# Two DRAM tables in turn for the block additions of a macaron layer, merged afterwards, and a new order of stages

## The chip, the core and the metric

The program runs on one core of a Trainium2 chip. The metric is device time in microseconds (us) of one execution, the median of the runs shown. The engines are named as in the profile: PE (TensorE, matrix products), DVE (VectorE), ACT (ScalarE), POOL (GpSimd, which here also issues the DMAs that add into memory or take row numbers) and SP (SyncE, which issues the plain DMAs).

## The reference

A layer in three parts on x of shape (4, 512, 512): half of a mixture of experts, an attention-like part with running sums over the sequence, and half of the same mixture again. Cut to what matters:

```python
x = x + 0.5 * ffn(layernorm(x))       # 8 experts, best 2 of each row, and a shared one
x = x + attn(layernorm(x))
x = x + 0.5 * ffn(layernorm(x))

# ffn: gates of the best two experts of a row
routed = sum_e gates[n, e] * (gelu(xf @ w1[e] + b1[e]) @ w2[e] + b2[e])
shared = gelu(xf @ sw1 + sb1) @ sw2 + sb2
# attn (batch of 512 rows, 32 heads, 8 angles of each): z = conv4(x @ W_mem), q = x @ W_q
# p = exp(score + decay); cs = cumsum([p, p*cos(k*theta), p*sin(k*theta)]); out = cs . q / den
# y = out_re @ W_re + out_im @ W_im; y = y_val * silu(y_gate); return y @ W_out
```

## The kernel before

All of it stands in one function, `macaron`. The four batches of 512 rows are walked as eight **jobs** q (four for the first mixture, four for the second) and four **groups** g of two batches (groups 0 and 1 belong to the first mixture, 2 and 3 to the second).

A job loads its rows (`fetch`), normalises them (`load`, `norm`), turns them for PE (`turn`, L722), makes the gate logits and ranks them, and computes the shared expert: `hidden` (L757) and then `acc` (L767, L769). `add_shared` (L1589) adds each tile of the shared result into the sum in DRAM, with an adding DMA from POOL.

A group then sends its 2048 (row, expert) pairs to 23 **blocks** of 128 pairs, each of one expert. `scatter` (L1557, 16 DMAs) writes the lists. Block j is brought by its row numbers into one of the NX = 2 tiles `xs` (`bring_rows`, L1569), turned (L801), multiplied by w1 (L810), turned again (L818), put through gelu on ACT (L991), multiplied by w2 (L826), scaled into one of two tiles `ys` (`keep_sums`, L1004) and added to its rows in DRAM by number (`add_rows`, L1582). Two blocks can hold the same row (a row has two experts), and so the additions of a group form a **chain**: `add_rows` of block j waits until that of block j-1 has landed, by the semaphore `y_added`, and the first of a group waits for the shared results. For the first mixture the table added to is `x1_rows` (which begins as a copy of x, L1803), for the second it is `out` (which begins as a copy of `x1_rows`, L1767, `begin_output`).

Between the mixtures stands attention, batch by batch. The head (`a_load` L1719, `a_stats`, `a_turn` L834, `a_mem` L845, `a_q` L854, `a_spread`) is followed by 16 steps on DVE (`c_turn`, `c_scan` L1374, `c_times` L1381 and L1386, `c_sum`), whose queries are loaded two steps ahead by SP into `qx` and whose sines come from ACT (L1072 to L1075); then `c_out` (L867), `o_gate` (L879) and `o_rows` (L888), whose tiles POOL adds into `x1_rows` (L1594). `kval` keeps the keys of 2 * HALVES = 4 halves.

Nothing is scheduled on the chip. `orders()` lays all stages of all engines in one order when the program is built: it runs a plan in which each `piece` has a length, the pieces that it comes after (with a time to landing for DMAs) and the banks that it needs, and takes for each engine the stage with the longest way to the end; the DVE steps come last among DVE's stages. Each engine's program is that order, with waits on semaphores. An engine that waits holds all that stands behind it.

## Time and profile before

| what | us |
|---|---|
| median of 3 runs (lowest, highest) | 1291.89 (1288.80, 1291.98) |
| the profiled execution, device time | 1298.13 |
| its span in the trace | 1296.8 |
| busy PE, DVE, ACT, POOL | 1005.9, 719.3, 594.9, 447.9 |

The profiled execution took 1.3 us beside its span, and was 6.2 us longer than the median. The profile page gives the busy time of each engine, the span in 40 slices, the chain of work that ended last (followed back from the last instruction through what released each step) and the costliest groups of instructions. The trace behind it gives each instruction with its start, and what ended the idle time before it. A share of busy time is an average over stages with different limits, and so the stages are read one by one: the blocks of group 0 (105 to 234 us), a long middle in which attention and groups 1 and 2 share the engines (to about 1045 us), the last attention product (to 1091 us), the last job (to 1152 us) and the blocks of group 3, alone, to the end.

### The profile page before, as it was taken

What the parts mean: (1) busy time and instruction counts of PE and PEld (TensorE: products, weight loads), DVE (VectorE), ACT (ScalarE), POOL (GpSimd) and SP (SyncE); (2) the same over time, 40 slices, a digit from 0 to 9 for tenths busy, and PEclk for the clock granted to TensorE, in tenths of its full rate; (3) what the DMA queues carried; (4) which work ended last, traced back from release to release, by engine and by line L of the source; (5) the groups of instructions that cost most, each with busy time, mean ns of one, the idle gap of its engine ahead of it and who ended that gap; (6) DMA issues with size and microseconds to landing.
All of it is one profiled execution on the core that took longest, in us unless ns stands there. A gap on an engine that the chain in (4) does not pass through costs nothing.

```text
span 1296.8 us, 10501 instructions
## 1 busy us (share of the span) xinstructions
PE 1005.9 (78%) x3168; PEld 538.4 (42%) x3168; DVE 719.3 (55%) x1162; ACT 594.9 (46%) x1015; POOL 447.9 (35%) x432
## 2 busy tenths in 40 slices
PE   6999889964986768887983569976986796969774
PEld 3446555422443434453431234454453442436542
DVE  3401000087888695987898989997996830200000
ACT  4334333333535575567532345376758720413332
POOL 4263443203634343232110134344452312244442
PEclk9999989986988897888896869988998998889997
DMA  8974554424156465486143742665676435035454
GB/s 283 377 188 87 101 86 69 78 84 124 30 108 177 95 124 107 105 234 157 49 111 85 175 139 47 153 151 129 124 189 146 78 49 106 33 74 96 92 90 55
DMA packets 60587, 155.13 MB, mean 120 GB/s; under 512 B 10962, under 2 KB 10962, under 8 KB 58358
## 3 DMA queue, kind: packets, MB, share of 16 engines
q0 software_dynamic: 29568, 60.90, 27.7%
q1 hardware_dynamic: 30966, 93.58, 23.8%
q8 instruction: 27, 0.44, 0.1%
q14 instruction: 26, 0.21, 0.1%
HBM read 99.74 MB, written 58.88 MB: 122 GB/s over the span
## 4 chain that ended last, share of the span: by engine, by line
DMA 32%; PE 32%; DVE 12%; ACT 8%; issue 7%; POOL 7%; SPq 1%; POOLq 0%; ACTq 0%; DVEq 0%
DMA x_rows<-ys,into_i 12%; DMA out_rows<-ys,into_i 11%; PE hps L757 6%; PE yps L769 6%; PE misc L888 4%; DMA xs<-x_normal,rows_i 4%; PE yps L826 3%; PE hps L810 3%; POOL slots L1557 3%; DVE run L1374 2%; PE misc L854 2%; DMA xin<-in_x 2%; ACT ys L1004 2%; PE misc L845 1%; ACT xin L1025 1%
## 5 line engine op out<-in xcount | busy, mean ns | idle before, releaser
L826 PE MATMUL yps<-w_all,hidden_sb 128*128 x368 | 202.5, 679 | 57.2 <-ACT hidden_sb L991 56.8
L810 PE MATMUL hps<-w_all,hidden_sb 128*128 x736 | 186.6, 400 | 1.2 <-ACT hidden_sb L974 1.1
L1374 DVE TENSOR_TENSOR_SCAN run<-pwx,trig 128x512 f32<-128x512 f32 x128 | 149.4, 1208 | 61.8 <-ACT trig L1075 61.3
L810 PEld LDWEIGHTS hps<-w_all,hidden_sb 128*128 128x128 f32 x736 | 145.4, 204 | 44.9 <-issue 27.4
L1569 POOL DMA_INDIRECT xs<-x_normal,rows_i x92 | 111.3, 1210 | 91.9 <-PE xps L801 65.2
L1004 ACT ACTIVATE ys<-yps,slots 128x512 f32<-128x512 f32 x92 | 62.9, 685 | 169.3 <-PE yps L826 72.3
L1582 POOL DMA_INDIRECT x_rows<-ys,into_i x46 | 79.4, 1727 | 169.6 <-ACT ys L1004 81.7
L1582 POOL DMA_INDIRECT out_rows<-ys,into_i x46 | 82.7, 1798 | 155.4 <-DMA out_rows<-ys,into_i 79.6
L826 PEld LDWEIGHTS yps<-w_all,hidden_sb 128*128 128x128 f32 x368 | 73.9, 213 | 128.7 <-issue 126.5
L757 PE MATMUL hps<-xnT,sw_sb 128*128 128x512 f32 x256 | 121.3, 623 | 3.2 <-ACT hidden_sb L964 1.7
L801 PE MATMUL xps<-ident,xs 128*128 128x128 f32 x368 | 60.7, 297 | 77.4 <-DMA xs<-x_normal,rows_i 75.9
L769 PE MATMUL yps<-sw_sb,hidden_sb 128*128 128x512 f32 x256 | 118.4, 605 | 0.0
L1557 POOL DMA_INDIRECT slots<-told,dest_i x64 | 70.1, 1096 | 63.0 <-DVE cmp_a L1244 28.2
L888 PE MATMUL misc<-turns_sb,tail_sb 128*128 128x512 f32 x192 | 86.8, 608 | 5.3 <-DVE tail_sb L1435 5.3
L722 PE MATMUL xps<-ident,xin 128*128 128x128 f32 x128 | 26.1, 359 | 80.5 <-ACT xin L1025 74.2
L801 PEld LDWEIGHTS xps<-ident,xs 128*128 128x128 f32 x368 | 45.9, 151 | 97.9 <-DMA xs<-x_normal,rows_i 59.2
L1381 DVE TENSOR_TENSOR trig<-run,qx 128x1024 f32<-128x1024 f32 x64 | 78.0, 1219 | 5.7 <-DMA qx<-q_cols 5.4
L1290 DVE BATCH_NORM_STATS2 stats_attn<-xin 128x6 f32<-128x512 f32 x16 | 10.6, 688 | 121.7 <-DMA xin<-x_rows 121.5
L1386 DVE TENSOR_TENSOR qx<-run,qx 128x1024 f32<-128x1024 f32 x64 | 77.9, 1217 | 0.0
L757 PEld LDWEIGHTS hps<-xnT,sw_sb 128*128 128x128 f32 x256 | 49.5, 200 | 67.4 <-issue 63.7
L1072 ACT ACTIVATE trig<-trig 128x512 f32<-128x512 f32 x64 | 40.4, 631 | 72.4 <-DVE trig L1363 72.2
L974 ACT COPY hidden_sb<-xps 128x512 f32<-128x512 f32 x92 | 53.1, 594 | 35.5 <-PE xps L801 33.9
(199 smaller groups left out, 1531.3 us busy)
## 6 DMA issues: line engine op xcount, KB each, us to landing
qx<-q_cols SPq DMA_DIRECT2D x128, 256.0 KB
x_normal<-xin SPq DMA_DIRECT2D x32, 256.0 KB, 3.8
w_all<-in_w_experts SPq DMA_DIRECT2D x8, 1024.0 KB, 9.8
xin<-x_rows SPq DMA_DIRECT2D x32, 256.0 KB, 6.5
turns_sb<-in_w_out SPq DMA_DIRECT2D x3, 1536.0 KB, 7.5
xin<-in_x SPq DMA_DIRECT2D x16, 256.0 KB, 4.2
x_rows<-ys POOLq DMA_DIRECT2D x16, 256.0 KB, 4.5
q_cols<-xin SPq DMA_DIRECT2D x16, 256.0 KB
```

Source lines behind the costliest of these rows:

```text
L757: t = PE.matmul(hps[:, bank, :], sw1_sb[:, c, n * P:(n + 1) * P], xnT[:, c, :], start=c == 0, stop=c == KC - 1)
L769: t = PE.matmul(yps[:, bank, :], hT[:, n, tb * P:(tb + 1) * P], sw2_sb[:, n, :], start=False, stop=n == SC - 1)
L801: t = PE.transpose(xps[:, bank, c * P:(c + 1) * P], xs[:, j % NX, c * P:(c + 1) * P], ident[:, :])
L810: t = PE.matmul(hps[:, bank, 0:H], xT[:, j % 2, c, :], w_all[:, bass.ds(expert[j] + c * H, H)], start=c == 0, stop=c == KC - 1)
L826: t = PE.matmul(yps[:, bank, :], hb[:, j % 2, ec, :], w_all[:, bass.ds(expert[j] + (KC * H + ec * D), D)], start=ec == 0, stop=ec == EC - 1)
L888: t = PE.matmul(misc[:, bank, :], yT[:, v, tb * P:(tb + 1) * P], wout_sb[:, v, :], start=v == 0, stop=v == VT - 1)
L1004: SE.activation(ys[:, j % 2, :], yps[:, bank, :], ACT.Copy, scale=slots[:, g % 2, j, 1:2]).then_inc(*ys_kept.of((g, j)))
L1374: t = VE.tensor_tensor_scan(run[:, c, :], pwx[:, n // M, :], trig[:, n % 2, c, :], 0.0, ALU.mult, ALU.add)
L1381: VE.tensor_tensor(trig[:, n % 2, :, :], run[:, :, :], qx[:, n % NQX, :, :], ALU.mult).then_inc(*real_made.of((b, n)))
L1557: GE.indirect_dma_start(slots_dram[g], bass.IndirectOffsetOnAxis(dest_i[:, g % 2, t, r:r + 1], 0), told[:, g % 2, t, r, :], None).then_inc ...
L1569: GE.indirect_dma_start(xs[:, j % NX, :], None, xn_rows[g % 2], bass.IndirectOffsetOnAxis(rows_i[:, g % 2, j:j + 1], 0)).then_inc(*xs_load ...
L1582: GE.indirect_dma_start(INTO[g], bass.IndirectOffsetOnAxis(into_i[:, g % 2, j:j + 1], 0), ys[:, j % 2, :], None, compute_op=ALU.add).then_ ...
```

## The change

**Two tables.** The even blocks of a group add into `x1_rows`, by `rows_i`, and the odd blocks into a second table, by `into_i`: the new `sum_rows` for the first mixture, `out` for the second. Each side has its own semaphore, and `add_rows` of block j waits for block j-2 instead of j-1. The shared results are no longer added: `store_shared` writes them, as plain stores from SP, as the first content of the second table. The copy of `x1_rows` to `out` is gone.

**Merging.** For attention each row tile is loaded from `x1_rows` as before, and then POOL adds the tile of `sum_rows` onto it in SBUF (`add_sums`, four DMAs a batch). `merge_rows` adds a batch of `sum_rows` into `x1_rows` for those who read it later (1 MB, from DRAM to DRAM). At the end of groups 2 and 3 `merge_output` adds the batches of `x1_rows` into `out`, one adding DMA of 1 MB a batch; the end of the program waits for them, and in group 3 the first odd block waits for the two of group 2.

**Room.** There are three `xs` tiles instead of two, so a block can be brought three ahead, and in exchange `kval` keeps three halves instead of four.

**The order.** The lengths in the plan are set anew. PE: `turn` and `a_turn` 0.8 to 0.7, `chunks` 1.6 to 1.3, `logits` 1.3 to 0.9, `acc` 4.4 to 4.2, `x` 0.8 and 2.0 to 0.7 and 1.9, `one` and `two` 2.0 to 1.9, `a_mem` 4.1 to 3.7, `a_q` 4.1 to 3.8, `a_spread` 1.2 to 0.8, `o_gate` 2.5 to 1.9, `o_rows` 5.5 to 5.3. POOL: `bring` 1.0 to 1.2, `add` 1.6 to 1.8 with a landing of 3.8 instead of 3.4. With the changed waits this moves instructions on every engine.

```diff
-        NX, NR = 2, 2
+        NX, NR = 3, 2
...
-        NK = 2 * HALVES
+        NK = 3
...
+        sum_rows = [nc.dram_tensor(f"sum_rows{i}", (GR + P, D), F32).ap() for i in range(2)]
...
-        SUM = [x1_rows if f == 1 else out for f, _ in JOBS]
-        INTO = [x1_rows[g] if g < 2 else out_rows for g in range(NG)]
+        SUM = [sum_rows if f == 1 else out for f, _ in JOBS]
+        INTO = [(x1_rows[g % 2], sum_rows[g % 2] if g < 2 else out_rows) for g in range(NG)]
...
-                piece("PE", s, 4.4, ("DVE", ("gT", q)), ("ACT", ("hidden", q, SC - 1)), *start[1:2],
+                piece("PE", s, 4.2, ("DVE", ("gT", q)), ("ACT", ("hidden", q, SC - 1)), *start[1:2],
...
-                piece("POOL", s, 1.0, ("ACT", s), ("SP", ("w_rows" if f == 1 else "w_out", b), 8.0))
+                piece("SP", s, 0.5, ("ACT", s), *([("POOL", ("add", g - 1, NB - 1), 3.8)] if g == NG - 1 else []))
...
-                piece("POOL", ("bring", g, j), 1.0, ("DVE", ("rows", g)), ("SP", ("norm", a), 2.5), ("SP", ("norm", z), 2.5),
+                piece("POOL", ("bring", g, j), 1.2, ("DVE", ("rows", g)), ("SP", ("norm", a), 2.5), ("SP", ("norm", z), 2.5),
...
-                last = [("POOL", ("add", g, j - 1), 3.4)] if j else []
-                if j == 0:
-                    last = [("POOL", ("acc", z, tb), 3.6) for tb in range(TB)]
-                    last += [("POOL", ("add", g - 1, NB - 1), 3.4)] if g else []
-                piece("POOL", ("add", g, j), 1.6, ("ACT", s), *last)
+                      ("POOL", ("add", g, j - 2), 3.8) if j >= 2 else ("SP", ("acc", z, TB - NR + j), 3.6))
+                if j >= 2:
+                    last = [("POOL", ("add", g, j - 2), 3.8)]
+                elif j == 1:
+                    last = [("SP", ("acc", q, tb), 3.6) for q in (a, z) for tb in range(TB)]
+                    last += [("POOL", ("m_out", b), 10.0) for b in range(GB)] if g == NG - 1 else []
+                else:
+                    last = [("SP", ("w_rows", JOBS[q][1]), 12.0) for q in (a, z)] if g < 2 else []
+                piece("POOL", ("add", g, j), 1.8, ("ACT", s), *last)
+            if g >= 2:
+                for q in (a, z):
+                    piece("POOL", ("m_out", JOBS[q][1]), 1.0, ("POOL", ("add", g, NB - 1), 3.8),
+                          ("POOL", ("add", g, NB - 2), 3.8))
...
+            for tb in range(TB):
+                piece("POOL", ("a_add", b, tb), 1.0, ("SP", ("a_load", b), 3.6 - 0.6 * (TB - 1 - tb)))
+            piece("POOL", ("m_rows", b), 1.0, ("POOL", ("a_add", b, TB - 1)))
+            piece("DVE", ("a_stats", b), 3.4, *[("POOL", ("a_add", b, tb), 3.8 - 0.8 * (TB - 1 - tb)) for tb in range(TB)])
...
+        def blocks_added(g):
+
+            return [y_added[side].at((g, NB - 1 - (NB - 1 - side) % 2)) for side in range(2)]
...
             def add_rows(g, j):
 
+                side = j % 2
                 pool.wait_ge(*ys_kept.at((g, j)))
-                if j > 0:
-                    pool.wait_ge(*y_added.at((g, j - 1)))
+                if j >= 2:
+                    pool.wait_ge(*y_added[side].at((g, j - 2)))
                 elif g > 0:
-                    pool.wait_ge(*y_added.at((g - 1, NB - 1)))
-                for i in range(NR):
-                    pool.wait_ge(*acc_added[i].at((GB * g + 1, TB - NR + i)))
-                GE.indirect_dma_start(INTO[g], bass.IndirectOffsetOnAxis(into_i[:, g % 2, j:j + 1], 0),
-                                      ys[:, j % 2, :], None, compute_op=ALU.add).then_inc(*y_added.of((g, j)))
-            def add_shared(q, tb):
-                f, b = JOBS[q]
-                pool.wait_ge(*acc_kept.at((q, tb)))
-                pool.wait_ge(*rows_begun[q].at(q))
-                GE.dma_start(row_tile(SUM[q], b, tb), ys[:, tb % NR, :],
-                             accum_op=ALU.add).then_inc(*acc_added[tb % NR].of((q, tb)))
+                    for end in blocks_added(g - 1):
+                        pool.wait_ge(*end)
+                if j == 0 and g < 2:
+                    for q in (GB * g, GB * g + 1):
+                        pool.wait_ge(*rows_begun[JOBS[q][1]].at(JOBS[q][1]))
+                elif j == 1:
+                    for i in range(NR):
+                        pool.wait_ge(*acc_stored[i].at((GB * g + 1, TB - NR + i)))
+                    if g == NG - 1:
+                        for b in range(GB):
+                            pool.wait_ge(*out_merged[b].at(b))
+                at = into_i if side else rows_i
+                GE.indirect_dma_start(INTO[g][side], bass.IndirectOffsetOnAxis(at[:, g % 2, j:j + 1], 0),
+                                      ys[:, j % 2, :], None, compute_op=ALU.add).then_inc(*y_added[side].of((g, j)))
+            def add_sums(b, tb):
+                pool.wait_ge(*a_loaded[tb].at(b))
+                pool.wait_ge(*blocks_added(b // GB)[1])
+                GE.dma_start(xin[:, tb, :], row_tile(sum_rows, b, tb), accum_op=ALU.add).then_inc(*a_summed[tb].of(b))
+            def merge_rows(b):
+                for tb in range(TB):
+                    pool.wait_ge(*a_loaded[tb].at(b))
+                GE.dma_start(batch_rows(x1_rows, b), batch_rows(sum_rows, b),
+                             accum_op=ALU.add, max_dma_last_dim=4096).then_inc(*rows_merged[b].of(b))
+            def merge_output(b):
+                for end in blocks_added(2 + b // GB):
+                    pool.wait_ge(*end)
+                GE.dma_start(batch_rows(out, b), batch_rows(x1_rows, b), accum_op=ALU.add,
+                             max_dma_last_dim=4096).then_inc(*out_merged[b].of(b))
...
-                sp.wait_ge(*y_added.at((b // GB, NB - 1)))
+                sp.wait_ge(*blocks_added(b // GB)[0])
...
-            def begin_output(b):
-                for i in range(2):
-                    sp.wait_ge(*row_added[i].at((b, TB - 2 + i)))
-                if b == B - 1:
-                    sp.wait_ge(*y_added.at((NG - 2, NB - 1)))
-                SP.dma_start(batch_rows(out, b), batch_rows(x1_rows, b)).then_inc(*rows_begun[B + b].of(B + b))
+            def store_shared(q, tb):
+                b = JOBS[q][1]
+                sp.wait_ge(*acc_kept.at((q, tb)))
+                if q == NJ - 1:
+                    for end in blocks_added(NG - 2):
+                        sp.wait_ge(*end)
+                SP.dma_start(row_tile(SUM[q], b, tb), ys[:, tb % NR, :]).then_inc(*acc_stored[tb % NR].of((q, tb)))
...
-                sp.wait_ge(*acc_added[i].at(acc_added[i].order[-1]))
-            sp.wait_ge(*y_added.at((NG - 1, NB - 1)))
+                sp.wait_ge(*acc_stored[i].at(acc_stored[i].order[-1]))
+            for end in blocks_added(NG - 1):
+                sp.wait_ge(*end)
+            for b in range(B):
+                sp.wait_ge(*out_merged[b].at(b))
```

POOL at the end of the program, before: the additions (L1582) stand all in `out_rows`.

```order
262 L1582 DMA out_rows<-ys,into_i 2048x512
263 L1569 DMA xs<-x_normal,rows_i 128x512
264 L1582 DMA out_rows<-ys,into_i 2048x512
265 L1569 DMA xs<-x_normal,rows_i 128x512
266 L1582 DMA out_rows<-ys,into_i 2048x512
267 L1569 DMA xs<-x_normal,rows_i 128x512
268 L1582 DMA out_rows<-ys,into_i 2048x512
269 L1569 DMA xs<-x_normal,rows_i 128x512 x2
270 L1582 DMA out_rows<-ys,into_i 2048x512 x6
```

The same place after (L1614 is `add_rows`, L1590 `bring_rows`, L1632 `merge_output`).

```order
293 L1614 DMA out_rows<-ys,into_i 2048x512
294 L1614 DMA x_rows<-ys,rows_i 1152x512
295 L1590 DMA xs<-x_normal,rows_i 128x512
296 L1614 DMA out_rows<-ys,into_i 2048x512
297 L1614 DMA x_rows<-ys,rows_i 1152x512
298 L1614 DMA out_rows<-ys,into_i 2048x512
299 L1614 DMA x_rows<-ys,rows_i 1152x512
300 L1614 DMA out_rows<-ys,into_i 2048x512
301 L1614 DMA x_rows<-ys,rows_i 1152x512
302 L1632 DMA out_rows<-x_rows 256x1024 x2
```

The two tables take turns, and two merges of 1 MB stand behind the last addition.

PE at the end of group 2, before: the w2 product of the last block (L826), then `hidden` of job 6 (L757) with `c_out` of the last attention half (L867) in its midst, then `acc` of job 6 (L767, L769) and `o_gate` (L879) in turn.

```order
1187 L826 MATMUL yps<-w_all,hidden_sb 128x512
1188 L757 MATMUL hps<-xnT,sw1_sb 128x512 x4
1189 L740 MATMUL xps<-chunk_sum,chunks_sb 128x8 x4
1190 L757 MATMUL hps<-xnT,sw1_sb 128x512 x4
1191 L867 MATMUL misc<-low_rows,rep_sb 128x512
1192 L757 MATMUL hps<-xnT,sw1_sb 128x512 x4
1193 L749 MATMUL xps<-ident,gcols 27x128 x4
1194 L757 MATMUL hps<-xnT,sw1_sb 128x512 x4
1195 L767 MATMUL yps<-bias_parts 128x512
1196 L769 MATMUL yps<-sw2_sb,hidden_sb 128x512 x4
1197 L879 MATMUL misc<-outT,wbd_sb 128x512
1198 L879 MATMUL xps<-outT,wbd_sb 128x512
```

The same place after, from the last block's product (L845) on: `hidden` is L776, `c_out` L886, `acc` L786 and L788.

```order
1195 L845 MATMUL yps<-w_all,hidden_sb 128x512
1196 L752 MATMUL xps<-xnT,gate_sb 32x512 x4
1197 L776 MATMUL hps<-xnT,sw1_sb 128x512 x8
1198 L759 MATMUL xps<-chunk_sum,chunks_sb 128x8 x4
1199 L776 MATMUL hps<-xnT,sw1_sb 128x512 x8
1200 L768 MATMUL xps<-ident,gcols 27x128 x4
1201 L886 MATMUL misc<-low_rows,rep_sb 128x512
1202 L786 MATMUL yps<-bias_parts 128x512
1203 L788 MATMUL yps<-sw2_sb,hidden_sb 128x512 x4
```

All of `hidden` now stands ahead of `c_out`, and all four tiles of `acc` stand ahead of the `o_gate` products, which come after the rows shown.

## Rows read from the trace of the kernel before

**Rows 1.** The page, part 4: the chain that ended last, by line.
```profile
DMA x_rows<-ys,into_i 12%; DMA out_rows<-ys,into_i 11%; PE hps L757 6%; PE yps L769 6%; PE misc L888 4%; DMA xs<-x_normal,rows_i 4%; PE yps L826 3%; PE hps L810 3%; POOL slots L1557 3%; DVE run L1374 2%; PE misc L854 2%; DMA xin<-in_x 2%; A
```
**Rows 2.** Timeline of POOL, additions of group 3: start us, us, engine, operation [idle <-releaser].
```profile
1167.38 1.65 POOL L1582 DMA_INDIRECT out_rows<-ys,into_i  x1 [2.30 <-ACT ys L1004]
...
1281.70 1.55 POOL L1582 DMA_INDIRECT out_rows<-ys,into_i  x1 [4.04 <-DMA out_rows<-ys,into_i]
...
1292.21 1.55 POOL L1582 DMA_INDIRECT out_rows<-ys,into_i  x1 [3.66 <-DMA out_rows<-ys,into_i]
```
**Rows 3.** Timeline of ACT, the last scaling of a block into ys.
```profile
1286.34 0.69 ACT L1004 ACTIVATE ys<-yps,slots 128x512 f32<-128x512 f32 x1 [4.62 <-DMA out_rows<-ys,into_i]
```
**Rows 4.** Groups by line in 1167 to 1290 us: count, busy us, mean ns, idle before, releasers.
```profile
L826 PE MATMUL yps<-w_all,hidden_sb 128*128 x88 | 42.1, 602 | 9.4 <-ACT hidden_sb L991 9.4
L1569 POOL DMA_INDIRECT xs<-x_normal,rows_i x18 | 17.9, 996 | 7.5 <-issue 4.9 <-PE xps L801 2.6
L801 PE MATMUL xps<-ident,xs 128*128 128x128 f32 x80 | 12.0, 285 | 12.1 <-DMA xs<-x_normal,rows_i 11.4 <-issue 0.6
```
**Rows 5.** Windows: stretch, its us, then busy (count) of PE, PEld, DVE, ACT, POOL, clock.
```profile
105.00:220.00 115.00, 99.84 (x391) 65.30 (x390) 3.57 (x24) 46.87 (x110) 51.36 (x39) 0.94 0.49 87
1156.70:1281.20 124.50, 102.56 (x414) 68.62 (x414) 0.00 (x0) 46.43 (x114) 52.69 (x41) 0.97 0.48 87
270.00:1045.00 775.00, 582.92 (x1735) 301.07 (x1734) 662.41 (x942) 424.87 (x675) 254.03 (x204) 0.87 0.52 122
```
**Rows 6.** Timeline of PE in group 3: one block without waits, and PE's last products.
```profile
1259.34 0.66 PE L801 MATMUL xps<-ident,xs 128*128 128x128 f32 x4 [1.59 <-DMA xs<-x_normal,rows_i]
1259.83 0.38 PE L818 MATMUL hps<-ident,hidden_sb 128*128 128x128 f32 x2
...
1263.49 0.38 PE L818 MATMUL hps<-ident,hidden_sb 128*128 128x128 f32 x2
...
1277.54 3.69 PE L826 MATMUL yps<-w_all,hidden_sb 128*128 x8 [0.31 <-ACT hidden_sb L991]
```
**Rows 7.** Timeline of POOL and ACT: two additions issued together, and who waited for each.
```profile
1144.45 1.94 POOL L1589 DMA_DIRECT2D out_rows<-ys  x2
...
1149.09 0.60 ACT L1018 ACTIVATE ys<-yps 128x512 f32<-128x512 f32 x1 [10.61 <-DMA out_rows<-ys]
1150.46 0.60 ACT L1018 ACTIVATE ys<-yps 128x512 f32<-128x512 f32 x1 [0.77 <-DMA out_rows<-ys]
```
**Rows 8.** DMA issues: operation, count, KB each, median us from issue to landing.
```profile
x_normal<-xin SPq DMA_DIRECT2D x32, 256.0 KB, 3.8
x_rows<-ys POOLq DMA_DIRECT2D x16, 256.0 KB, 4.5
x_rows<-in_x SPq DMA_DIRECT2D x4, 15.0
out_rows<-x_rows SPq DMA_DIRECT2D x4, 8.2
```
**Rows 9.** Timeline of PE after group 0; attention's loads: durations ns, first and last start.
```profile
219.85 13.90 PE L757 MATMUL hps<-xnT,sw_sb 128*128 128x512 f32 x32
...
246.66 0.60 PE L834 MATMUL misc<-ident,xin 128*128 128x128 f32 x4
...
L1719 SPq DMA_DIRECT2D xin<-x_rows x16: 319/379/387, 233.7 to 762.7; - x16
```
**Rows 10.** Waits of DVE in 394 to 620 us: total us, times, longest.
```profile
DVE run L1374 <- ACT trig L1075: 37.2, 9, 11.9
DVE trig L1381 <- DMA qx<-q_cols: 3.7, 1, 3.7
```
**Rows 11.** Timeline after group 2: PE's hidden and last attention product, DVE's last step.
```profile
1031.10 3.60 PE L757 MATMUL hps<-xnT,sw_sb 128*128 128x512 f32 x8
...
1069.71 20.76 PE L888 MATMUL misc<-turns_sb,tail_sb 128*128 128x512 f32 x48
...
1044.79 1.38 DVE L1419 SCALAR_TENSOR_TENSOR tail_sb<-outT,small_sb,misc 128x512 f32<-128x512 f32 x2
```

95 lines of the change are left out of this document (52 added, 43 removed).

## The prediction

> **What bounds the kernel now.** I read the chain that ended last first [rows 1]: 12% of the span is additions into x_rows on their way to landing, 11% additions into out_rows, some 300 us of 1296.8. No engine has such a share. It lies mostly in groups 0 and 3, where little or nothing of attention runs beside the blocks.
>
> The last blocks show the mechanism. The 23 additions of group 3 start 5.67 us apart (22 intervals in 1292.21 - 1167.38 [rows 2]). Of this an addition takes 4.6 us from its start to landing at the very end (the one from 1281.70 lets ACT go at 1286.34 [rows 2, 3]); ACT's copy into ys, 0.69 [rows 3], or as much time on POOL, passes until the next begins, some 0.8 in all, so a landing is 4.9 on average. What PE needs itself is far less. At 1259 to 1263 us [rows 6] it runs a block without a wait: 0.49 us for the turning (1259.34 to 1259.83) and 3.66 from one L818 to the next (which holds L818, L810 and L826), so **4.15 us a block** against 5.67. It was done at 1281.2, while the additions ended at 1296.8 [rows 2, 6]. The time in groups 0 and 3 is that of the chain.
>
> In the middle DVE is busy 662.4 of 775 us and PE 582.9 [rows 5]. There DVE is the tightest engine, and a chain that gets shorter gives back only what DVE idles for.
>
> **Group 3, additions in two tables.** Two additions may be under way at once. A pair then needs one landing and one ACT copy: 4.9 + 0.8 = 5.7 us for two blocks, 2.85 a block. POOL needs 1.6 for an addition, 1.0 for a bring and two gaps of 0.3 (4.9 us for issue ahead of the brings), together 3.2 [rows 2, 4]. Both lie under PE's 4.15, so PE is late next. Its waits in this stretch were 11.4 us for the brought rows and 9.4 us for gelu [rows 4]. The third xs tile and the freed POOL take the first away; the second (9.4 / 22 = 0.43 a block) I keep, since gelu still stands between two products of a block. That is 4.15 + 0.43 = 4.58 us a block. PE's busy time over the same 23 blocks is 102.6 / 23 = 4.46 [rows 5], more than 4.15 because in a run with gaps the end of each piece counts; 4.46 + 0.43 = 4.89. I take the middle, **4.7**. Before, PE took 124.5 us for the 23 blocks [rows 5]; after, 23 x 4.7 = 108.1, a gain of 16.4. Behind PE the additions took 15.6 us (1281.2 to 1296.8); now one copy (0.1 + 0.69) and one landing (4.6), 5.4, a gain of 10.2. **Sum 26.6.** Bounds: at 4.15 a block 39; at 5.1 (if the new order of PE meets ACT more often) 17.
>
> Do two additions really overlap? Two of the shared additions were issued 0.97 us apart (1.94 for two) [rows 7]; those who waited went on at 1149.09 and 1150.46, 1.37 us apart and not a landing of 4.6.
>
> **The last merge.** New, behind everything: two adding DMAs of 1 MB from DRAM to DRAM, after a wait on POOL (0.8). No row has it. The nearest is the plain copy of the same 1 MB between the same tables, 8.2 us [rows 8]. The adding form costs the same as the plain one at 256 KB (4.5 with POOL's longer issue, against 3.8) [rows 8]. From 256 KB to 1 MB, 4.4 us more for 0.75 MB is 5.9 us a MB, so the second merge adds 5.9: 0.8 + 8.2 + 5.9 = **15 us lost.** Bounds: both hidden in one another, 9; each like the slowest kind of 1 MB copy in the trace, 15.0 [rows 8], one after the other, 31. I take 15, because the chip does nothing else then, as at the 8.2.
>
> The Trainium skill, DMA: Bandwidth & Descriptors, section Anatomy of one DMA, has for a DMA issued by GpSimd 2.0 us and then 436 KB a us, an estimate of 6.8 us for these 2 MB. By it the sum would be 8 us better. The trace speaks against it: the 1 MB copy took 8.2 where the rule has 4.4 [rows 8].
>
> **Group 0.** The same chain, but PE had other work among the blocks: it was busy 99.8 of 115 us and idle 15.2 [rows 5], and right behind it stand hidden and acc of job 2, on PE alone, from 219.85 until attention's rows are turned (the first at 246.66) [rows 9]. So only PE's idle counts. I keep a third of it: **gain 10** (5 to 15). The new add_sums (about 4.5 us, like the 256 KB addition [rows 8]) stands between the last addition and attention's first row. It is hidden: PE has 26.8 us of hidden and acc from the end of the blocks to the first turned row, while a copy and landing (5.4), add_sums (5) and the 13 us from attention's first load (233.7) to that row [rows 9] make 23.4. If that cover went, it would cost up to 5.
>
> **Shared results, copies, kval.** The 32 shared additions leave POOL (about 1 us each, mostly in its idle time) and become stores on SP; four copies of 1 MB go and four merge_rows come, off the path. A third kval half makes a_mem of half 1 wait for steps of the batch before, which PE's order already has behind them. I cost these at nothing; the cover of all three is DVE's 85% busy middle.
>
> **The middle.** Between 394 and 620 us DVE waited 37.2 us for ACT's sines [rows 10]; ACT stood in order behind the blocks. A shorter chain takes part of that, but the same ACT work is packed closer. I take 4 us (-12 to 30). At the end of group 2 hidden ran only from 1031.10, the end of the blocks, and the last attention product began at 1069.71, while DVE was done at 1046.2 [rows 11]. PE had 38 us of work, of which hidden (four times 3.6) would fit ahead of DVE's end if the blocks end sooner. Up to 14 us; DVE limits it as well, I take 4. **Gain 8.**
>
> **The sum.** 26.6 - 15 + 10 + 8 = 29.6 us. Against the profiled execution, 1298.1 - 29.6 = 1268.5; that was 6.2 above the median, so 1291.9 - 29.6 = 1262.3, say **1262**.
>
> **Rivals.**
> 1. The middle gives much: DVE's 37.2 us mostly return, 30 instead of 4, and group 3 runs at 4.4 a block (7 us). 1262 - 26 - 7 = **1229**. For it: a third of the chain on the additions lies in the middle. Against: DVE at 85%.
> 2. The gain in the middle is eaten. The new order was laid for other lengths than those under load, and add_sums stands in three more heads: between 0 and -12 for the middle instead of 8, which gives 1270 to 1282, and **1282** at the end. For it: POOL and DMA are slower there than at the ends.
> 3. The merges cost 31 and more and the middle gives nothing: 1291.9 - 26.6 - 10 + 31 = **1286**, and from 33 us on it is no change.
> 4. Slower, by SP's queue. The shared stores now stand among the query loads in SP's order, and each waits for ACT's copy of a product of PE. If PE is late, the load behind is late and with it DVE. Twelve such stores (jobs 3, 4 and 5) stand in the middle, and a load is about one step of DVE ahead. The wait for queries is 3.7 us today [rows 10]. It decides when the twelve hold DVE for more than 34 / 12 = 2.8 us each; at 4 us, 1262 + 48 = **1310**.
> 5. The change doesn't do what it says: additions of one queue land one after another whatever the semaphore. Then groups 0 and 3 keep 5.67 us and the merges come on top: 1291.9 + 15 - 8 = **1299**. The pair in [rows 7] speaks against it.
>
> **Chances.** Forecast (1248 to 1274) 0.56; rival 1 (below) 0.14; rival 2 (above, to 1284) 0.18; rival 3 0.04; rival 4 0.05; rival 5 0.03. A measurement of this kernel can tell about 0.3%, 3.9 us, from no change. Faster by more: 0.56 + 0.14 + 0.18 and half of rival 3, 0.90; within 0.02; slower 0.08. The range goes from the middle of rival 1 and the forecast to the end of rival 2: 1240 to 1284.
>
> **What would show it.** Additions of group 3 starting less than 4.8 us apart, in pairs of tables, with PE's wait for xs gone and its last product some 5 us before the last landing; at the end two merges of together about 15 us; PE's end of group 0 at about 210 instead of 220; the wait of DVE for trig below 37 us. The prediction is wrong if PE's own waits for ACT grow with the new order, if the merges cost 30, or if DVE shows new waits for qx.

## The result, and the profile after

The changed kernel took **1239.45 us** (1235.05 to 1244.39, 4 runs) against 1290.35 for the kernel before beside it: a ratio of 0.961 (95% interval 0.956 to 0.966), 50.9 us less. The forecast was 1262, 29.6 less, with a range from 1240: the direction was right and the gain was forecast much too small. The profiled execution took 1235.89 us, with a span of 1234.6.

The page of the changed kernel, the chain that ended last by engine and by line:

```profile
PE 46%; DVE 15%; DMA 12%; ACT 12%; POOL 7%; issue 7%; SPq 1%; POOLq 0%; DVEq 0%; ACTq 0%
PE yps L845 10%; PE hps L829 9%; PE hps L776 7%; PE yps L788 6%; PE misc L907 6%; POOL slots L1578 4%; DVE run L1395 2%; DMA outT<-tail_sb 2%; DMA x_rows<-tail_sb 2%; PE misc L873 2%; DMA x_rows<-ys,rows_i 2%; ACT xin L1045 2%; DVE trig L1402 1%; DMA q_cols<-xin 1%; PE misc L864 1%
```

The additions on their way to landing, 23% of the span in [rows 1], are down to some 2%. What stands first now is PE's work on the blocks, L845 and L829 (L826 and L810 before).

The timeline of POOL in group 3: start, us, engine and line, operation, and in brackets the idle time before it with its releaser.

```profile
1118.34 1.64 POOL L1614 DMA_INDIRECT x_rows<-ys,rows_i  x1 [3.69 <-ACT ys L1023]
...
1123.24 1.58 POOL L1614 DMA_INDIRECT out_rows<-ys,into_i  x1 [1.97 <-ACT ys L1023]
...
1127.66 1.58 POOL L1614 DMA_INDIRECT x_rows<-ys,rows_i  x1 [0.30 <-issue]
...
1216.47 1.55 POOL L1614 DMA_INDIRECT x_rows<-ys,rows_i  x1 [1.91 <-ACT ys L1023]
1221.67 1.93 POOL L1632 DMA_DIRECT2D out_rows<-x_rows  x2 [3.65 <-DMA x_rows<-ys,rows_i]
```

Against [rows 2]: tables in turn, and 4.46 us from one addition to the next (22 intervals in 1216.47 - 1118.34) instead of 5.67. From the first block to the merges' issue POOL's additions wait 31.6 us for ACT's copy and only 5.3 for a landing; before it was 34.8 and 31.9. The end is new: the two merges are issued at 1221.67 and the span ends at 1234.6, 12.9 us later. POOL had waited for the last addition up to then.

Four stretches of the changed kernel, then three of the kernel before. Columns: stretch, its us, then busy us (count) of PE, PEld, DVE, ACT, POOL, the granted clock, DMA share, GB/s.

```profile
89.97:200.17 110.20, 105.05 (x445) 69.94 (x443) 0.00 (x0) 49.97 (x119) 54.49 (x42) 1.00 0.58 104
227.49:997.32 769.83, 583.15 (x1795) 303.99 (x1794) 659.84 (x939) 419.17 (x676) 260.40 (x209) 0.89 0.55 130
997.32:1108.06 110.74, 85.14 (x228) 37.98 (x226) 25.94 (x74) 24.35 (x36) 24.32 (x31) 0.91 0.27 64
1108.06:1215.47 107.41, 100.30 (x414) 67.90 (x414) 0.00 (x0) 47.42 (x114) 54.50 (x43) 0.98 0.59 105
```
```profile
92.33:219.85 127.52, 110.03 (x435) 72.22 (x434) 3.57 (x24) 51.22 (x119) 55.14 (x43) 0.93 0.49 88
246.66:1030.75 784.09, 590.95 (x1756) 304.07 (x1755) 659.35 (x919) 423.93 (x677) 253.02 (x205) 0.87 0.52 121
1030.75:1156.72 125.97, 99.37 (x266) 44.91 (x264) 26.48 (x92) 31.15 (x44) 34.26 (x40) 0.91 0.34 63
```

The stretches are: group 0's blocks on PE; attention's first turned row to DVE's last scan; that scan to group 3's first block; group 3's blocks. Group 3's is 124.5 us before [rows 5].

**Where the gain lies.** I cut every profiled execution at four marks: PE's first block product of group 0 (x), its first turn of attention's rows (a), the start of DVE's last scan, and group 3's first block product (x3). All in us; the last column is PE's busy time from the last scan to x3.

| kernel | x | x to a | a to last scan | last scan to x3 | x3 to end | PE busy, scan to x3 |
|---|---|---|---|---|---|---|
| before | 92.3 | 154.3 | 784.1 | 126.0 | 140.1 | 99.4 |
| changed | 90.0 | 137.5 | 769.8 | 110.7 | 126.5 | 85.1 |
| changed, second execution | 92.5 | 137.6 | 769.8 | 111.6 | 127.6 | 85.1 |
| no_last_merge | 96.7 | 137.6 | 765.6 | 110.8 | 113.5 | 85.6 |
| merge_8k | 93.9 | 137.5 | 768.8 | 114.4 | 127.0 | 88.8 |
| ties_early | 97.1 | 137.2 | 770.2 | 111.2 | 127.0 | 82.3 |
| ties_late | 92.9 | 137.1 | 768.2 | 129.4 | 125.7 | 103.1 |
| tables_old_lengths | 94.0 | 133.5 | 765.7 | 132.5 | 125.1 | 109.0 |
| two_xs_own_order | 96.7 | 138.4 | 765.9 | 133.2 | 128.0 | 107.9 |
| four_xs_two_kval | 94.4 | 137.5 | 763.4 | 123.6 | 126.7 | 99.6 |
| two_xs_same_order | 93.6 | 155.3 | 826.0 | 112.2 | 141.4 | 86.3 |
| tables_one_chain | 95.2 | 157.4 | 792.9 | 112.5 | 151.5 | 85.9 |
| order_only | 96.0 | 155.2 | 788.7 | 130.7 | 143.5 | 102.6 |
| before_acc_last | 92.5 | 154.6 | 773.8 | 125.1 | 139.7 | 103.3 |
| before_less_hidden6 | 93.0 | 156.7 | 772.0 | 122.8 | 142.4 | 93.2 |
| after_acc_last | 93.7 | 137.5 | 766.0 | 114.6 | 126.1 | 86.8 |
| after_less_hidden6 | 94.6 | 137.6 | 765.8 | 117.6 | 127.1 | 92.3 |

before_acc_last and before_less_hidden6 have the order of the kernel before up to the last scan; no_last_merge, merge_8k, after_acc_last and after_less_hidden6 have that of the changed one. They show what one execution is worth: a to last scan is 772 to 784 before and 766 to 770 after. With the means of such twins the gains are: x to a 155.2 to 137.6, **17.6**; a to last scan 776.6 to 767.6, **9.0**; last scan to x3 126.0 (one execution only) to 111.9 (the four that have no edit there), **14.1**; x3 to end 140.7 to 126.9, **13.8**. Together 54.5, less 1.0 for a later x. The profiled pair shows 62.2, mostly because that execution of before was long in the middle (784.1, its twins 773.8 and 772.0) and that of the changed kernel began its blocks early (x at 90.0, the mean is 93.6). The medians say 50.9; the 2.6 us between that and the marks are within what single executions differ by.

### The profile page after: what moved, and what is told of

Its sections match the earlier page's. It is cut to its first block, busy times and chain, and to the rows that moved or that the text cites. A ratio compares the mean times of both kernels' runs of the same rounds, so it can differ in the third digit from the quotient of the medians.

```text
span 1234.6 us, 10515 instructions
## 1 busy us (share of the span) xinstructions
PE 970.2 (79%) x3168; PEld 525.8 (43%) x3168; DVE 719.1 (58%) x1162; ACT 586.2 (47%) x1008; POOL 441.7 (36%) x424
## 4 chain that ended last, share of the span: by engine, by line
PE 46%; DVE 15%; DMA 12%; ACT 12%; POOL 7%; issue 7%; SPq 1%; POOLq 0%; DVEq 0%; ACTq 0%
PE yps L845 10%; PE hps L829 9%; PE hps L776 7%; PE yps L788 6%; PE misc L907 6%; POOL slots L1578 4%; DVE run L1395 2%; DMA outT<-tail_sb 2%; DMA x_rows<-tail_sb 2%; PE misc L873 2%; DMA x_rows<-ys,rows_i 2%; ACT xin L1045 2%; DVE trig L1402 1%; DMA q_cols<-xin 1%; PE misc L864 1%
## 5 line engine op out<-in xcount | busy, mean ns | idle before, releaser
L845 PE MATMUL yps<-w_all,hidden_sb 128*128 x368 | 180.8, 614 | 32.7 <-ACT hidden_sb L1010 32.7
L829 PE MATMUL hps<-w_all,hidden_sb 128*128 x736 | 176.5, 383 | 4.2 <-ACT hidden_sb L993 4.2
L829 PEld LDWEIGHTS hps<-w_all,hidden_sb 128*128 128x128 f32 x736 | 138.7, 192 | 52.6 <-issue 38.0
L1395 DVE TENSOR_TENSOR_SCAN run<-pwx,trig 128x512 f32<-128x512 f32 x128 | 149.3, 1207 | 19.0 <-ACT trig L1095 18.5
L1590 POOL DMA_INDIRECT xs<-x_normal,rows_i x92 | 107.5, 1168 | 137.2 <-PE xps L820 105.3
L776 PE MATMUL hps<-xnT,sw_sb 128*128 128x512 f32 x256 | 122.3, 627 | 4.8 <-ACT xnT L961 2.7
L788 PE MATMUL yps<-sw_sb,hidden_sb 128*128 128x512 f32 x256 | 120.4, 614 | 0.0
L1614 POOL DMA_INDIRECT x_rows<-ys,rows_i x48 | 82.4, 1717 | 72.3 <-ACT ys L1023 67.4
L845 PEld LDWEIGHTS yps<-w_all,hidden_sb 128*128 128x128 f32 x368 | 67.7, 194 | 95.1 <-issue 93.0
L1578 POOL DMA_INDIRECT slots<-told,dest_i x64 | 76.9, 1201 | 58.5 <-DVE cmp_a L1264 30.0
L1638 POOL DMA_DIRECT2D x_rows<-tail_sb x16 | 14.4, 900 | 202.1 <-ACT tail_sb L1062 202.1
L1175 DVE MAX8 most<-xps 128x8 f32<-128x8 f32 x32 | 3.1, 159 | 138.5 <-PE xps L759 138.4
L776 PEld LDWEIGHTS hps<-xnT,sw_sb 128*128 128x128 f32 x256 | 49.7, 201 | 69.2 <-issue 63.5
L1001 ACT COPY hidden_sb<-hps 128x256 f32<-128x256 f32 x92 | 34.2, 372 | 79.6 <-PE hps L829 79.6
L788 PEld LDWEIGHTS yps<-sw_sb,hidden_sb 128*128 128x128 f32 x256 | 46.8, 193 | 55.4 <-issue 55.4
L993 ACT COPY hidden_sb<-xps 128x512 f32<-128x512 f32 x92 | 54.2, 591 | 29.6 <-PE xps L820 24.8
```

What stands on the lines that cost most here:

```text
L776: t = PE.matmul(hps[:, bank, :], sw1_sb[:, c, n * P:(n + 1) * P], xnT[:, c, :], start=c == 0, stop=c == KC - 1)
L788: t = PE.matmul(yps[:, bank, :], hT[:, n, tb * P:(tb + 1) * P], sw2_sb[:, n, :], start=False, stop=n == SC - 1)
L829: t = PE.matmul(hps[:, bank, 0:H], xT[:, j % 2, c, :], w_all[:, bass.ds(expert[j] + c * H, H)], start=c == 0, stop=c == KC - 1)
L845: t = PE.matmul(yps[:, bank, :], hb[:, j % 2, ec, :], w_all[:, bass.ds(expert[j] + (KC * H + ec * D), D)], start=ec == 0, stop=ec == EC - 1)
L1395: t = VE.tensor_tensor_scan(run[:, c, :], pwx[:, n // M, :], trig[:, n % 2, c, :], 0.0, ALU.mult, ALU.add)
L1578: GE.indirect_dma_start(slots_dram[g], bass.IndirectOffsetOnAxis(dest_i[:, g % 2, t, r:r + 1], 0), told[:, g % 2, t, r, :], None).then_inc ...
```

## The experiments

### The overlap of the additions

**tables_one_chain**: everything of the change, but each addition also waits for the one before it in the other table.

```diff
                 at = into_i if side else rows_i
+                if j >= 1:
+                    pool.wait_ge(*y_added[1 - side].at((g, j - 1)))
```


> The changed kernel in its own order, with one more wait: an addition also waits until the one before it in the other table has landed. So the tables, merges, tiles and order stay, and only the overlap of two additions goes. Theory chain: group 3 goes back to 5.7 us an addition (27 us lost), group 0 loses 15 to 19, the middle some more: 1285 to 1305, at or above the kernel before, since the merge of 13 us stays. Theory order: the middle keeps its gain, so only groups 0 and 3 lose, 1275 to 1285.

Measured: 1311.14 us, ratio 1.016 (1.013 to 1.019), above both expectations. The last additions of group 3 on POOL, and ACT's longest waits in group 0 (total us, times, longest):

```profile
1280.79 1.55 POOL L1616 DMA_INDIRECT x_rows<-ys,rows_i  x1 [4.13 <-ACT ys L1023]
1286.33 1.55 POOL L1616 DMA_INDIRECT out_rows<-ys,into_i  x1 [4.00 <-DMA x_rows<-ys,rows_i]
1291.56 1.55 POOL L1616 DMA_INDIRECT x_rows<-ys,rows_i  x1 [3.67 <-DMA out_rows<-ys,into_i]
```
```profile
ACT ys L1023 <- DMA x_rows<-ys,rows_i: 26.4, 7, 4.8
...
ACT ys L1023 <- DMA sum_rows<-ys,into_i: 14.3, 7, 3.1
```

The spacing is back at 5.4 us and the waits for a landing are back. This one wait is worth 72 us (1311.1 against 1239.5), and the table says where: 20 from x to a, 23 from a to the last scan, 25 from x3 to the end, 2 between. Rival 5 of the prediction, that additions of one queue land one after another anyway, is gone. So is the thought that the middle has little of the chain. The stretch from the last scan to x3, however, keeps its gain without the overlap (112.5): that gain belongs to the order. DVE's waits for the scans' sines (ACT) in this middle stretch, of this kernel, the changed one and the one before:

```profile
DVE run L1395 <- ACT trig L1095: 39.5, 15, 6.2
```
```profile
DVE run L1395 <- ACT trig L1095: 18.5, 12, 6.2
```
```profile
DVE run L1374 <- ACT trig L1075: 57.6, 15, 11.9
```

**order_only**: the kernel before with all new lengths in its planner, one table.

```diff
-                piece("PE", s, 2.0, ("ACT", ("x", g, j)),
+                piece("PE", s, 1.9, ("ACT", ("x", g, j)),
...
```


> The kernel before with all the new lengths in its plan (PE's stages, bring 1.2, add 1.8 and its landing 3.8), one table, one chain, two xs tiles: the order alone. Theory chain (nearly all of the gain comes from two additions under way at once): within 8 us of the kernel before, 1282 to 1298, since the additions of groups 0 and 3 stay 5.7 us apart. Theory order (the 30 us that were not forecast, in the middle and at its end, come from lengths that fit the chip): 15 to 30 us faster than before, 1260 to 1275, with the last attention product starting 15 us or more earlier than 1069.7 and the blocks of group 3 as long as before (about 140 us from the first turned block to the end).

Measured: 1309.32 us, ratio 1.013 (1.008 to 1.017), outside both expectations. With one table the new lengths cost 19 us, 12 of them from a to the last scan (788.7 against 776.6).

**tables_old_lengths**: the changed kernel with the old lengths.

```diff
-                piece("PE", s, 1.9, ("ACT", ("x", g, j)),
+                piece("PE", s, 2.0, ("ACT", ("x", g, j)),
...
```


> The changed kernel with the old lengths in its plan (the waits and the tables are the new ones). Theory chain: 1240 to 1250, within 10 us of the changed kernel's 1239. Theory order: 1255 to 1275, with the loss before the last attention product, which would start 15 us or more later than 1024.7; the blocks of group 3 take the same as in the changed kernel, about 127 us with the merge, under both.

Measured: 1250.78 us, ratio 0.969 (0.965 to 0.973), 11 us behind the changed kernel and 0.8 above the upper end of the first expectation. Group 0 and the middle are even a little shorter; all that it lacks, and more, lies between the last scan and x3: 132.5 against 110.7.

### The third xs tile

**two_xs_same_order**: two tiles, each engine's order exactly that of the changed kernel.

```diff
-        NX, NR = 3, 2
+        NX, NR = 2, 2
...
-                earlier_x = [("PE", ("x", g, j - NX))] if j >= NX else [("PE", ("x", g - 1, NB - 1))] if g else []
+                earlier_x = [("PE", ("x", g, j - 3))] if j >= 3 else [("PE", ("x", g - 1, NB - 1))] if g else []
```


> Edit: the changed kernel with two xs tiles instead of three, in exactly the order of the changed kernel on every engine. Theory (the overlap of the additions carries the gain, the third xs tile little): PE's rate in groups 0 and 3 falls by 0 to 0.3 us a block, 0 to 7 us in each of them, 1240 to 1250. Rival (the third tile is needed for PE's pace): PE waits for the brought rows as before (11.4 us in group 3) in groups 0 and 3, 1258 and more. If POOL's bring, which then waits for the tile's last reader, holds up the additions queued behind it, ACT waits for ys as before.

Measured: 1321.07 us, ratio 1.022 (1.016 to 1.028). The theory was far too low; the rival had only "1258 and more", with the mechanism of its last sentence. POOL's longest wait in group 3 (total us, times, longest), and its longest single one:

```profile
POOL xs L1590 <- PE xps L820: 47.0, 13, 6.7
```
```profile
1240.56 0.95 POOL L1590 DMA_INDIRECT xs<-x_normal,rows_i  x1 [6.68 <-PE xps L820]
1241.82 1.62 POOL L1614 DMA_INDIRECT out_rows<-ys,into_i  x1 [0.30 <-issue]
```

POOL works in order. The bring of block j+2 now waits for PE's turning of block j, and the addition queued behind it is issued late although its data is there: ACT had written it by 1235.07 (1234.38 + 0.69), and it was issued at 1241.82. Groups 0 and 3 lose what the overlap had given (155.3, 141.4). The middle loses more than that, 826.0 against 792.9 with one chain; there the same wait comes to 217.8 us.

**two_xs_own_order**: two tiles and the planner told so.

> Edit: the changed kernel with two xs tiles, and the order laid for two (the planner told of two). With two tiles in the order laid for three the bring of a block waited 47 us for PE in group 3 and 50 in group 0, the additions behind it on POOL came late, and the kernel took 1321. Theory A (the order laid for three was what two tiles could not follow; two tables are what gives the gain): groups 0 and 3 run at 4.7 to 5.0 us a block, 1245 to 1262. Theory B (without the third tile the two tables give nothing, since bring, PE's turning and the addition still form one chain through POOL): 5.3 us a block and more, 1290 to 1320.

Measured: 1264.61 us, ratio 0.977 (0.972 to 0.982). Groups 0 and 3 run almost as fast as with three tiles (138.4 and 128.0). So the two tables carry the gain of these groups, and a tile is needed only by an order that counts on it. Of the 25 us that this kernel lacks, 22.5 are again from the last scan to x3 (133.2); they put it 3 us above the first expectation.

**four_xs_two_kval**: four tiles, and two kval halves to make room.

```diff
-        NX, NR = 3, 2
+        NX, NR = 4, 2
...
-        NK = 3
+        NK = 2
```


> Edit: the changed kernel with four xs tiles and two kval halves (the memory allows no more), the order laid for these. In the changed kernel PE waits 0.3 us a block in groups 0 and 3 for ACT and POOL's bring waits 12 to 19 us for PE, but PE does not wait for xs behind the first block. Theory (three tiles are enough): groups 0 and 3 within 2 us of the changed kernel; the rest by the order and by a_mem, which waits for all steps of the batch before: 1238 to 1260. Rival (each tile more frees POOL's order further): 1225 to 1236.

Measured: 1248.99 us, ratio 0.967 (0.962 to 0.971). The groups are those of the changed kernel to 0.2 us (137.5 and 126.7): three tiles are enough. The 10 us that this kernel lacks come with its order: 123.6 from the last scan to x3.

### The last merges

**no_last_merge**: the final merges of batches 2 and 3 are left out.

```diff
             def merge_output(b):
+                if b >= GB:
+                    return
...
-            for b in range(B):
+            for b in range(GB):
                 sp.wait_ge(*out_merged[b].at(b))
```


> The changed kernel without the two merges at the very end (batches 2 and 3 of the output lack their even blocks and the attention rows): the price of the last merge by itself. If it stands wholly behind the last addition, the time is 13 us less than the changed kernel, about 1226. If the program's end would wait for something else anyway (the odd additions, the stores), less than 6 us are gained.

Measured: 1225.31 us, ratio 0.950 (0.948 to 0.952): the merges cost 14.1 us on the medians and 13.4 from x3 to the end (126.9 to 113.5).

**merge_8k**: the same merges in pieces of 8 KB.

```diff
-                             max_dma_last_dim=4096).then_inc(*out_merged[b].of(b))
+                             max_dma_last_dim=8192).then_inc(*out_merged[b].of(b))
```


> Edit: the changed kernel, but each of the two last merges is split into pieces of 8 KB instead of 4 KB. In the changed kernel they took 12.9 us for 2 MB from the issue to the end of the span. If the cost lies in the pieces (512 of them), it falls by 2 to 5 us, to 1234 to 1237; if it lies in the bytes moved and added, within 1 us of 1239; with eight pieces for each of 16 engines an uneven spread may cost 1 to 3 us.

Measured: 1240.93 us, ratio 0.961 (0.956 to 0.966), no change; x3 to end 127.0. Half as many pieces cost the same, so the cost is not in their number, as far as these two sizes tell.

### From DVE's last scan to group 3's first block

Here is what the table kept pointing at. PE in the changed kernel:

```profile
983.32 7.13 PE L776 MATMUL hps<-xnT,sw_sb 128*128 128x512 f32 x16
...
991.10 7.11 PE L776 MATMUL hps<-xnT,sw_sb 128*128 128x512 f32 x16
...
1000.72 3.70 PE L788 MATMUL yps<-sw_sb,hidden_sb 128*128 128x512 f32 x8
...
1012.89 3.70 PE L788 MATMUL yps<-sw_sb,hidden_sb 128*128 128x512 f32 x8
1016.42 1.02 PE L898 MATMUL misc<-outT,wbd_sb 128*128 128x512 f32 x2
...
1024.69 20.84 PE L907 MATMUL misc<-turns_sb,tail_sb 128*128 128x512 f32 x48 [2.80 <-DVE tail_sb L1456]
1058.43 1.97 PE L741 MATMUL xps<-ident,xin 128*128 128x128 f32 x8 [12.90 <-ACT xin L1045]
```

Against [rows 11]: the hidden products of job 6, 14 us of PE, lie ahead of the last scan (997.32; all but their last 0.9 us) and not behind it (1031.10 against 1030.75). From there on PE works nearly without a gap in both kernels until o_rows, so what was done ahead is missing behind. The first idea was that the four acc products ahead of o_gate hold the end.

**before_acc_last** and **after_acc_last**: in each kernel, the acc products of job 6 come after the last o_rows product.

```diff
                 piece("PE", s, 4.2, ("DVE", ("gT", q)), ("ACT", ("hidden", q, SC - 1)), *start[1:2],
+                      *([("PE", ("o_rows", B - 1, TB - 1))] if q == NJ - 2 else []),
                       bank=[("yps", ("ACT", s))])
```


> Edit: the same in the kernel before: its four acc products of job 6 come after the last o_rows product of batch 3. There PE works without a gap from 1031.10 (0.3 us behind the last scan) to o_rows at 1069.71, 38.6 us, the four acc 16.8 us of it; DVE had done its last step at 1046.2. Theory (PE holds the end of group 2 in both kernels, so the changed kernel's 11.6 us less from the last scan to o_rows came from group 2's blocks ending 22 us earlier against DVE and not from DVE): o_rows starts 22 to 28 us after the last scan instead of 39, and of that 10 to 16 us about 8 to 12 stay in the time (job 7's rows wait 12.7 us behind it): 1278 to 1283. Rival (DVE holds it as well, as the prediction had it): o_rows moves by 4 us or less, and the time by less than 4: 1286 to 1291.

> Edit: the changed kernel, but the four acc products of job 6 come after the last o_rows product of batch 3 instead of ahead of its o_gate products; all else keeps its order. In the changed kernel PE works without a gap from its hidden of job 6 (14 us ahead of DVE's last scan) to o_rows at 1024.69, of which the four acc (1000.3 to 1016.4) are 16.1 us, while DVE had done its last step at 1008.8 and waited 10.36 us for the gates. After o_rows PE waited 12.9 us for job 7's rows. Theory (PE, not DVE, holds the end of group 2): o_rows starts 5 to 6 us earlier (about 21.5 us after the last scan instead of 27.4), the acc products fill PE's later wait of 12.9 us, and the time falls by 3 to 6 us, to about 1234 to 1237. Rival (DVE and the move of outT by DMA hold it): o_rows within 1.5 us of 27.4 after the last scan and 1239 to 1243.

Measured: 1287.23 us, ratio 0.995 (0.992 to 0.999), and 1243.78 us, ratio 0.965 (0.959 to 0.971). PE ahead of o_rows in the first of them (last scan at 1020.96), then in the second (997.23):

```profile
1042.17 1.10 PE L880 MATMUL misc<-outT,wbd_sb 128*128 128x512 f32 x2 [2.94 <-DMA outT<-tail_sb]
...
1050.36 2.13 PE L889 MATMUL misc<-turns_sb,tail_sb 128*128 128x512 f32 x3 [2.80 <-DVE tail_sb L1436]
```
```profile
1013.06 2.05 PE L899 MATMUL misc<-outT,wbd_sb 128*128 128x512 f32 x2 [13.45 <-DMA outT<-tail_sb]
...
1022.86 22.54 PE L908 MATMUL misc<-turns_sb,tail_sb 128*128 128x512 f32 x48 [2.80 <-DVE tail_sb L1457]
```

In the kernel before, o_rows came 29.4 us after the last scan instead of 39.0: PE had held it there, not DVE. But x3 came only 0.9 us sooner. The same 16.8 us of PE then stand behind o_rows, where they fill a wait: PE is idle 4.8 us less. But it is also busy 3.9 us longer with the same products (103.3 against 99.4, the o_rows products 22.53 against 20.76). The theory was right on who holds o_rows and wrong on the price: 3.6 us on the medians, of 8 to 12 expected, and the interval of the ratio leaves 1 to 11. In the changed kernel the theory failed: PE ran into DVE's own way at once (13.45 us for outT), o_rows gained 1.8 instead of 5 to 6, and the time is the rival's. There the two are nearly level. Moving PE's work within the stretch gives little or nothing; work done ahead of the last scan leaves it. The table has this as a rule: last scan to x3, less PE's busy time, is 21.8 to 29.7 us in all 17 executions, while the two go from 111 to 133 and from 82 to 109.

**before_less_hidden6** and **after_less_hidden6**: three quarters of the hidden products of job 6 are left out.

```diff
-                for c in range(KC):
+                cs = KC // 4 if q == 6 else KC
+                for c in range(cs):
...
-                                  start=c == 0, stop=c == KC - 1)
+                                  start=c == 0, stop=c == cs - 1)
```


> Left out: three quarters of each hidden product of job 6 (the shared expert's first layer for batch 2 of the second feed-forward), 10.8 of its 14.4 us of PE; the order and all waits are as in the kernel before. In the kernel before PE runs these products from 1031.10, right behind DVE's last scan (1030.75). Theory (from the last scan to group 3's first block the time is PE's remaining work and some 26 us of waits, in which order whatever; the changed kernel has these products ahead of the last scan, and that is its 15.3 us in this stretch): from the last scan to group 3's first block 126.0 becomes 114 to 118, and the time falls by 8 to 11 us, to 1280 to 1283. Rival (the stretch is held by DVE, the move of outT and the chain of job 7's rows): it falls by 4 us or less, to 1287 or more.

> Left out: the same three quarters of the hidden products of job 6, in the changed kernel. There 14 us of them lie ahead of DVE's last scan (997.3), and DVE's own way to o_rows (last step, move of outT, gates, sines) allows it from 25.6 us after the last scan at the earliest; it is at 27.4. Theory (PE's work left after the last scan decides down to DVE's way): PE comes to wait for DVE, and only 0 to 4 us stay in the time: 1236 to 1240. Rival (PE holds the stretch throughout): 8 to 11 us less, 1229 to 1232.

Measured: 1283.32 us, ratio 0.991 (0.987 to 0.995), 9.6 us less on the medians, of the 8 to 11 expected; and 1244.30 us, ratio 0.962 (0.957 to 0.966), not faster at all. The medians are on the theory's side in the first, but its profile is not: there the stretch is 122.8, only 3.2 us shorter, where the theory had 114 to 118 and the rival 4 or less. PE's busy time fell by 6.2 and not by 10.8, at a granted clock of 0.86 instead of 0.91, and its idle time grew by 3.1. So this pair does not settle the size; the next one does. In the second the time is no lower, which speaks against the rival, though it is 4 us above the theory's range too. Why the second gained nothing is told at the end.

**ties_late** and **ties_early**: tables, tiles, waits and lengths of the changed kernel; only the planner's priorities are shaken by up to 1 and 2 us, so that near ties fall otherwise.

```diff
+            rnd = 1392
+            for k in work:
+                rnd = rnd * 1103515245 + 12345 & 2147483647
+                way[k] += 1.0 * (rnd >> 16 & 1023) / 1024
```


> Edit: the changed kernel, its tables, tiles, waits and lengths; only the planner's priorities get up to 1 us each from a fixed sequence of numbers, so that near ties fall otherwise. In the order that comes out, PE ends group 2's blocks later against DVE's last steps, hidden of job 6 lies wholly behind the last scan, and its acc products alternate with o_gate, as in the kernel before. Theory (PE's work left after DVE's last scan decides this stretch, and the order alone sets it): from the last scan to group 3's first block 122 to 128 us instead of 111 to 114, nothing else moved by more than 3, 1247 to 1256. Rival (the gain there is due to the tables or to POOL's freed time): within 4 us of the changed kernel, 1236 to 1243.

> Edit: the same with up to 2 us each and another sequence: PE ends group 2's blocks earlier still, about 10 us more ahead of DVE's last scan than in the changed kernel, at the price of a last scan some 4 us later. Theory (PE's work left after the last scan decides only down to DVE's own way, 25.6 us from the last scan to o_rows): 0 to 6 us less from the last scan to group 3's first block, 2 to 6 us more ahead of it, 1235 to 1242. Rival (it goes on by PE's work alone): 8 to 10 us less behind the last scan, 1230 to 1234.

Measured: **1254.04** us, ratio 0.972 (0.966 to 0.977), and 1239.73 us, ratio 0.960 (0.955 to 0.966). PE in ties_late, whose last scan starts at 998.21:

```profile
997.43 5.40 PE L780 MATMUL hps<-xnT,sw_sb 128*128 128x512 f32 x8 [1.91 <-ACT xnT L965]
...
1009.15 7.11 PE L780 MATMUL hps<-xnT,sw_sb 128*128 128x512 f32 x16
...
1029.63 3.70 PE L792 MATMUL yps<-sw_sb,hidden_sb 128*128 128x512 f32 x8
1033.17 1.02 PE L902 MATMUL misc<-outT,wbd_sb 128*128 128x512 f32 x2
...
1038.94 3.60 PE L911 MATMUL misc<-turns_sb,tail_sb 128*128 128x512 f32 x8
```

and the same stretch of ties_late and of ties_early as windows:

```profile
998.21:1127.61 129.40, 103.07 (x273) 45.78 (x271) 26.46 (x93) 30.37 (x43) 28.79 (x34) 0.88 0.29 66
```
```profile
1004.47:1115.65 111.18, 82.31 (x211) 36.55 (x209) 23.07 (x69) 22.62 (x33) 24.31 (x31) 0.86 0.23 59
```

ties_late differs from the changed kernel by 2 us at most in the three other stretches between the marks, and by 18 in this one: hidden of job 6 begins 0.8 us ahead of the last scan and lies behind it, as in the kernel before. With nothing changed but near ties the place of group 2's blocks against DVE's last steps is worth 11 to 15 us of the whole. ties_early put them 8 us further ahead (the last w2 product starts at 979.53, 24.9 us ahead of the last scan, against 16.9) and gained nothing: there DVE's way holds o_rows, which comes 24.4 us after the last scan against 27.4 and takes 22.54 us against 20.84.

**after_again**: the changed kernel beside them.

> The changed kernel once more, beside the two, for a second profiled execution and more timed ones. From the twins of both kernels that have the same order up to DVE's last scan I expect its last scan at 997 to 1001 and the time at 1237 to 1243; the ratio to the kernel before 0.958 to 0.965.

Measured: 1242.65 us (1236.4 to 1245.53, 6 runs), ratio 0.963 (0.958 to 0.968), last scan at 999.88. No kernel here is faster than the changed one with all its work in it; ties_early is its equal.

## Why the prediction fell short, point by point

Two steps of the sum failed: in group 0 "so only PE's idle counts", and at the end of group 2 "DVE limits it as well, I take 4". The middle was sized too small as well.

- **Group 3, 26.6: right.** PE took 107.4 us for 23 blocks, 4.67 a block against 4.7 (17.1 us against 16.4); the last addition was issued 1.0 us after PE's end (1215.47 to 1216.47), and the merges were issued 5.2 us behind that, against 5.4 in all. In the profiled pair the gain up to the merges' issue is 26.5 (140.1 less 1221.67 - 1108.06). PE's wait for the brought rows is gone behind the first block, as forecast. Of the waits in [rows 4] PE's for gelu fell further than the forecast had it, from 9.4 to 2.7 (groups by line, 1108 to 1222 us), and what PE needs without waits is 4.36 a block (100.30 / 23), a little over the 4.15 of the one block I had read. The forecast took the middle of 4.58 and 4.89, and that it fits to 0.03 a block is partly luck:

```profile
L829 PE MATMUL hps<-w_all,hidden_sb 128*128 x184 | 44.9, 387 | 1.9 <-ACT hidden_sb L993 1.9
L845 PE MATMUL yps<-w_all,hidden_sb 128*128 x92 | 43.8, 599 | 2.7 <-ACT hidden_sb L1010 2.7
```

- **The last merge, -15: right.** It measured 13.4 to 14.1. One reason given for the size does not hold: the four plain copies with their 8.2 were issued from 571.9 to 1095.6 us, beside attention and the last job, and not while "the chip does nothing else". The Trainium skill (DMA: Bandwidth & Descriptors, section Anatomy of one DMA) gives an estimate of 6.8 for these bytes. The measurement decides, and it is twice that.
- **Group 0, 10: mis-sized, 17.6 measured.** The step that failed is "so only PE's idle counts". The idle went from 17.5 us (127.52 - 110.03) to 5.2 (110.20 - 105.05), 12.3 instead of 10. But PE's busy time also fell, by 5.0, with the granted clock from 0.93 to 1.00, although this stretch now holds one tile of acc more, about 4 us of products that stood ahead of x before. tables_one_chain, with the changed kernel's order and the same products, has 110.6 busy at 0.95 and 17.2 idle, so it is the overlap that brings both. Gaps cost twice: as gaps, and in the products behind them. The cover named for add_sums held: PE was idle 0.9 us in all between the last block and attention's first row.
- **Shared results, copies, kval, 0: right but for one place.** In [rows 7] POOL's additions of job 7 waited for ACT between the scatter and the bring (from 1143.49 + 0.95 to 1152.51, 8.1 us). Now nothing of the kind stands there, and the bring follows 5.1 us after the scatter:

```profile
1098.58 0.96 POOL L1578 DMA_INDIRECT slots<-told,dest_i  x1 [0.30 <-issue]
1104.62 0.99 POOL L1590 DMA_INDIRECT xs<-x_normal,rows_i  x1 [5.09 <-DVE into_i L1305]
```

- **The middle up to the last scan, 4: 9.0 measured**, within its bounds. DVE's busy time is the same (659.4 and 659.8), so it is idle time. The wait for sines fell from 57.6 to 18.5, and others grew by more than half of that, among them those for the block lists (2.1 to 10.4) and for attention's rows, which now come with add_sums (3.1 to 7.9). The overlap as such gives 23 there, and the order takes 12 to 16 back (tables_one_chain and order_only have 793 and 789, against 777). The 4 had neither term at this size, and that it lay within 5 of the 9.0 is partly luck. Rival 2 had the mechanism of the loss; rival 4 did not occur, no wait for qx is left.
- **The end of group 2, 4 of "up to 14": 14.1 measured, the largest miss.** The failed step is "DVE limits it as well, I take 4". In the kernel before DVE had 9.6 us to spare there (before_acc_last), and in every kernel the stretch is PE's remaining work and 22 to 30 us of idle time. The prediction saw the 14.4 us of hidden that "would fit ahead of DVE's end", and then took less than a third. Nor does the overlap bring it: tables_one_chain has none and 112.5. It is the order that places the hidden products. What the prediction could not take from the rows was whether the new order would do so: two_xs_own_order, tables_old_lengths and ties_late have the same additions and keep 129 to 133. But the order of the changed kernel could be read before the run, and it had them there.

The misses are 7.6, 5.0 and 10.1 us, and 2.2 from x3 to the end, less 1.0: the 24 between forecast and traces (21 on the medians).
